# Four PSUM banks that rotate over attention units, with scores and turned probabilities of a unit in the same bank

## The reference

```python
qkv = (x @ w_qkv.T + b_qkv).reshape(B, T, 3, H, dh)
...
std_logits = jnp.einsum('bhqd,bhkd->bhqk', q, k) * scale
...
incidence = jnp.einsum('bqhp,bkhp->bhqk', read_lines, J_write)
...
weights = decays[:, None, None] ** diffs_pos[None] * past[None].astype(x.dtype)
bias = incidence * weights[None] * bias_scale[None, :, None, None]
logits = std_logits + bias
...
logits = jnp.where(causal_mask[None, None], -jnp.inf, logits)
attn = jax.nn.softmax(logits, axis=-1)
out = jnp.einsum('bhqk,bhkd->bqhd', attn, v).reshape(B, T, D)
return out @ w_out.T + b_out
```

## Time and profile before

| | |
|---|---|
| median of 3 runs | 3171.58 us (3170.65 to 3173.0) |
| the profiled execution: its time | 3169.16 us |
| the profiled execution: its span, first to last instruction | 3167.4 us |
| mean clock granted to PE | 0.789 of full speed |
| PE, DVE, ACT, POOL busy over the span | 76%, 49%, 33%, 26% |
| attention iterations | eight, from about 190 to 2085 us |

### The profile page before, as it was taken

The page is one execution under the profiler, slowest core; times in us unless marked ns, Lnnn a source line. Parts: engine busy times, 40 slices in busy tenths (PEclk is TensorE's granted clock), DMA queues, the critical chain, the costliest instruction groups (busy, mean ns, idle before and its releaser), DMA issues. The chain is left out here.

```text
span 3167.4 us, 33541 instructions
## 1 busy us (share of the span) xinstructions
PE 2413.1 (76%) x11754; PEld 1587.2 (50%) x11754; DVE 1562.1 (49%) x3728; ACT 1037.9 (33%) x2567; POOL 830.2 (26%) x583
## 2 busy tenths in 40 slices
PE   6258877777777767877777777855999597979798
PEld 5134444444444444544444444533777357574747
DVE  2468567466565765745755754422000144444443
ACT  2024343343343334334234334321222151515050
POOL 0435243153153134225224321020000223232220
PEclk9567886877777677688688688677999797979787
DMA  3000100110020010010020010022222302020200
GB/s 144 35 15 1 55 21 1 42 43 1 10 75 1 9 58 18 9 56 21 1 64 21 1 55 21 1 69 82 90 90 90 103 1 65 3 59 9 56 12 14
DMA packets 66386, 120.48 MB, mean 38 GB/s; under 512 B 29621, under 2 KB 43947, under 8 KB 63795
## 3 DMA queue, kind: packets, MB, share of 16 engines
q1 hardware_dynamic: 53434, 76.51, 7.2%
q0 software_dynamic: 12800, 41.95, 4.8%
HBM read 97.36 MB, written 21.07 MB: 37 GB/s over the span
## 5 line engine op out<-in xcount | busy, mean ns | idle before, releaser
L1022 ACT ACTIVATE att_buf<-att_buf,nmin 128x384 f32<-128x384 f32 (+3 forms) x512 | 288.3, 563 | 854.2 <-DVE nmin L1344 854.0
L858 PE MATMUL bank<-kk,qT 32*128 32x512 f32 (+2 forms) x1024 | 352.7, 725 | 92.1 <-DVE nmin L1344 92.0
L690 POOL TENSOR_TENSOR big<-ex_at,kx 128x2048 f32<-128x2048 f32 x64 | 236.6, 3705 | 428.1 <-DVE xt_na L1131 354.3
L885 PE MATMUL bank<-ident,att_buf 128*128 128x128 f32 x1280 | 254.0, 339 | 22.3 <-ACT att_buf L1030 19.2
L639 POOL TENSOR_TENSOR big<-kx 128x1280 f32<-128x1280 f32 x64 | 162.7, 2570 | 311.1 <-ACT kx L957 303.2
L1131 DVE TENSOR_REDUCE xt_na<-big 128x64 f32<-128x1024 f32 x128 | 240.8, 1899 | 2.2 <-POOL big L690 1.6
L1333 DVE TENSOR_TENSOR att_buf<-bank,wdiag 128x128 f32<-128x128 f32 x384 | 93.0, 284 | 288.9 <-PE bank L863 286.2
L899 PE MATMUL bank<-att_buf,vp 128*32 128x128 f32 x2560 | 234.0, 323 | 0.0
L1030 ACT COPY att_buf<-bank 128x384 f32<-128x384 f32 (+3 forms) x512 | 208.8, 410 | 21.8 <-PE bank L899 17.3
L885 PEld LDWEIGHTS bank<-ident,att_buf 128*128 128x128 f32 x1280 | 187.2, 179 | 33.8 <-ACT att_buf L1022 23.1
L858 PEld LDWEIGHTS bank<-kk,qT 32*128 32x128 f32 x1024 | 117.4, 234 | 165.7 <-DVE nmin L1344 124.5
(11 more groups left out here) (333 smaller groups left out, 4525.1 us busy)
## 6 DMA issues: line engine op xcount, KB each, us to landing
ew<-in_eW SPq DMA_DIRECT2D x16, 1024.0 KB, 8.4
buf_d<-gac SPq DMA_DIRECT2D x16, 320.0 KB, 2.8
eb<-buf_d SPq DMA_DIRECT2D x8, 640.0 KB, 3.6
y_d<-yy SPq DMA_DIRECT2D x8, 640.0 KB, 10.7
xt_na<-in_xT SPq DMA_DIRECT2D x8, 512.0 KB, 3.6
nA<-in_xN SPq DMA_DIRECT2D x8, 512.0 KB, 4.4
x_d<-x SPq DMA_DIRECT2D x8, 512.0 KB, 4.2
kf<-x_d SPq DMA_DIRECT2D x8, 512.0 KB, 3.2
```

Of the source, the lines that this page charges most:

```text
L690: pool.tensor_tensor(pv[:, :, c * P:(c + 1) * P].rearrange("p o (h d) -> p o h d", d=DH), spread(ex[:, t, :, 8 * c:8 * c + 8], 3, DH), spr ...
L858: pe.matmul(bank[u % 2][:, 0:n], qT[r:r + 32, g, i * P:(i + 1) * P], kk[r:r + 32, g, T * i * P:T * i * P + n], start=True, stop=False)
L885: mm = pe.transpose(bank[3 + u % 2][:, j * P:(j + 1) * P], pr[:, u % NPR, j * P:(j + 1) * P], ident[:])
L1022: act.activation(pr[:, u % NPR, 0:n], pr[:, u % NPR, 0:n], ACT.Exp, scale=-1.0, bias=nmin[:, u % 4:u % 4 + 1], accum_out=rsum[:, i, h:h + ...
```

## The change

Two banks for scores and two for turned probabilities become one ring of four, rot(u) = bank[(0, 1, 3, 4)[u % 4]]. The scores of unit u go to rot(u); when DVE has read them, turn(u) writes the turned probabilities of the same unit to the same bank. The bank is free for unit u + 4 when ACT has copied it, so scores(u) now waits for prT_ok in place of max_ok, and turn(u) loses its own wait for prT_ok.

The orders on the engines change with it. On PE: turn(k), side work, scores(k+2), values(k); scores of pairs 0 and 1 are issued ahead of the loop. On ACT: both exps of pair k, both turned of pair k, side work. On DVE the order is kept, with one more wait, for its own minima of the pair before. raw_out(0) on ACT is called one pair sooner in the count (u = 30), the sums' steps on PE stand at the end of their pair, and values of the last pair stand ahead of turn_sums(1).

```diff
--- before.py
+++ after.py
@@ -541,6 +541,8 @@
                 sm = sb("sm", [P, 16, T])
                 gi = sb("gi", [P, 4, T])
 
+                ROT = (0, 1, 3, 4)
+                rot = lambda u: bank[ROT[u % 4]]
                 units = [(2 * (2 * d + x) + c, i) for d in range(H // 4) for i in (3, 0, 2, 1) for c in range(2) for x in range(2)]
                 N = len(units)
                 long_before = [sum(i == T - 1 for _, i in units[0:u]) for u in range(N)]
@@ -567,13 +569,15 @@
                                 while pair[1] is not None and pair[1] <= slot:
                                     pair[1] = next(pair[0], None)
 
-                        def interleave(unit, streams):
+                        def interleave(unit, streams, unit_end=lambda u: None):
 
                             for u in range(0, N, 2):
                                 if b2 is not None:
                                     unit(u)
                                 advance(streams, u)
                                 advance(streams, u + 1)
+                                if b2 is not None:
+                                    unit_end(u)
                             assert all(due is None for _, due in streams)
 
                         with nc.Block() as block:
@@ -841,7 +845,7 @@
                                     g, r = row_of(u)
                                     k = long_before[u]
                                     if k >= 2:
-                                        pe.wait_ge(s("inc_used"), k - 1)
+                                        pe.wait_ge(s("inc_used"), k - k % 2)
                                     if k % 2:
                                         pe.wait_ge(s("inc_mm"), k)
                                     if u == N // 2 + 4 * T:
@@ -855,18 +859,18 @@
                                     i = units[u][1]
                                     g, r = row_of(u)
                                     n = min(i + 2, T) * P
-                                    pe.matmul(bank[u % 2][:, 0:n], qT[r:r + 32, g, i * P:(i + 1) * P],
+                                    pe.matmul(rot(u)[:, 0:n], qT[r:r + 32, g, i * P:(i + 1) * P],
                                               kk[r:r + 32, g, T * i * P:T * i * P + n], start=True, stop=False)
 
                                 def mask(u):
                                     i = units[u][1]
-                                    pe.matmul(bank[u % 2][:, i * P:(i + 1) * P], identb[:], negb[:], start=False, stop=True)\
+                                    pe.matmul(rot(u)[:, i * P:(i + 1) * P], identb[:], negb[:], start=False, stop=True)\
                                         .then_inc(s("score_mm"), 1)
 
                                 def scores(u):
 
-                                    if u >= 2:
-                                        pe.wait_ge(s("max_ok"), u)
+                                    if u >= 4:
+                                        pe.wait_ge(s("prT_ok"), u - 2)
                                     if units[u][1] == T - 1:
                                         incidence(u)
                                     logits(u)
@@ -879,10 +883,8 @@
                                 def turn(u):
                                     h, i = units[u]
                                     pe.wait_ge(s("exp_ok"), u + 1)
-                                    if u >= 2:
-                                        pe.wait_ge(s("prT_ok"), u - 1)
                                     for j in range(i + 1):
-                                        mm = pe.transpose(bank[3 + u % 2][:, j * P:(j + 1) * P], pr[:, u % NPR, j * P:(j + 1) * P], ident[:])
+                                        mm = pe.transpose(rot(u)[:, j * P:(j + 1) * P], pr[:, u % NPR, j * P:(j + 1) * P], ident[:])
                                     mm.then_inc(s("turn_mm"), 1)
 
                                 def values(u):
@@ -914,12 +916,13 @@
                                     pe.matmul(bank[2][:], sel[:], rT, start=True, stop=True).then_inc(s("rb_mm"), 1)
 
                                 def unit(u):
-                                    if u + 2 < N:
-                                        scores(u + 2)
                                     turn(u)
                                     turn(u + 1)
-                                    if u:
-                                        values(u - 2)
+
+                                def unit_end(u):
+                                    if u + 4 < N:
+                                        scores(u + 4)
+                                    values(u)
                                     if u == N // 2 + 4:
                                         turn_sums(0)
                                     if u == N // 2 + 6:
@@ -933,10 +936,10 @@
                                 if b2 is not None:
                                     turn_features()
                                     scores(0)
-                                interleave(unit, side)
+                                    scores(2)
+                                interleave(unit, side, unit_end)
                                 if b2 is not None:
                                     turn_sums(1)
-                                    values(N - 2)
                                     broadcast_sums(1)
 
                                     pe.wait_ge(s("att_ok"), 2)
@@ -1027,7 +1030,7 @@
                                     act.wait_ge(s("turn_mm"), u + 1)
                                     if u >= 3:
                                         act.wait_ge(s("val_mm"), (u - 3) // 2 + 1)
-                                    act.copy(prT[:, u % 3, 0:n], bank[3 + u % 2][:, 0:n]).then_inc(s("prT_ok"), 1)
+                                    act.copy(prT[:, u % 3, 0:n], rot(u)[:, 0:n]).then_inc(s("prT_ok"), 1)
 
                                 def raw_out(c):
 
@@ -1039,11 +1042,11 @@
                                     act.copy(rT, bank[2][0:H // 2, :]).then_inc(s("rT_ok"), 1)
 
                                 def unit(u):
-                                    for x in (u, u + 1):
-                                        if x + 2 < N:
-                                            exps(x + 2)
-                                        turned(x)
-                                    if u == N // 2:
+                                    exps(u)
+                                    exps(u + 1)
+                                    turned(u)
+                                    turned(u + 1)
+                                    if u == N // 2 - 2:
                                         raw_out(0)
                                     if u == N // 2 + 4:
                                         sums_out(0)
@@ -1073,9 +1076,6 @@
                                             last = act.activation(blocks(g, at, n), tiles_of(src, n), ACT.Copy, scale=fack[:, g, v:v + 1])
                                         last.then_inc(s("qkT_ok0"), 1)
                                 advance(side, -1)
-                                if b2 is not None:
-                                    exps(0)
-                                    exps(1)
                                 interleave(unit, side)
                                 if b2 is not None:
                                     sums_out(1)
@@ -1323,8 +1323,10 @@
                                     i = units[u][1]
                                     n = (i + 1) * P
                                     dve.wait_ge(s("score_mm"), u + 2)
+                                    if u:
+                                        dve.wait_ge(s("max_ok"), u)
                                     for x in range(2):
-                                        h, lg = units[u + x][0], bank[(u + x) % 2]
+                                        h, lg = units[u + x][0], rot(u + x)
                                         db = dpad[:, x * T * P:x * T * P + P]
                                         if i == T - 1:
                                             k = long_before[u + x] % 2
@@ -1333,7 +1335,7 @@
                                             dve.tensor_tensor(db, lg[:, n:n + P], wdiag[:, h, :], ALU.mult).then_inc(s("db_ok"), 1)
                                     tiled = lambda ap: ap.rearrange("p (j k) -> p j k", k=P)
                                     for x in range(2):
-                                        lg, dst = bank[(u + x) % 2], pr[:, (u + x) % NPR, 0:n]
+                                        lg, dst = rot(u + x), pr[:, (u + x) % NPR, 0:n]
                                         if i == T - 1:
                                             dve.wait_ge(s("inc_used"), long_before[u + x] + 1)
                                         else:
```

## The result

The kernel became slower: 3219.81 us median (3210.08 to 3232.01, 4 runs) against 3171.11 us (3164.23 to 3173.0, 4 runs); the ratio is 1.016, 95% interval 1.0121 to 1.0198. The forecast was 3154 us with a range of 3118 to 3195: the time moved the other way and lies above the range. In the changed kernel the lines stand two to four lower: scores are L862 (was L858), incidence L854 (L850), masks L867 (L863), turns L887 (L885), values L901 (L899), exponentials L1025 (L1022), copies L1033 (L1030), minima L1346 (L1344), turned router rows L767 (L763).

The account below looks back on a forecast made before the run. Attention was taken as bound by a chain alternating between PE and DVE, no engine full. Middle iterations -25, first +6, last +1 sum to -18 us: 3151.2 from the profiled 3169.2, 3154 as median; range 3118 to 3195.

Parts of the forecast that it names:

- What it adds (1): Pairs without PE side work: PE waits for ACT's copies before the next scores, 0.57 us each.
- Seven or eight of the 17 lie under DVE's stretch and cost nothing: Middle iteration: of 17 pairs without PE side work, those where DVE is full add nothing; the other 9 cost 5 us.
- the broadcast: Sums' broadcast (L914) on PE comes later; DVE waits 1.3 to 3.4 us for it in its full stretch, 2.5 taken.
- What it saves: Attention: scores no longer wait for the pair before's biases, some 1.5 us saved at one pair; iteration start gains about 1.4.
- The walk of the middle iteration: Operations of 657 to 863 us replayed in the new order at old durations: 4.1 us saved, 25 over six iterations.
- The first iteration: Attention without router: 22 us of turnarounds and other additions replace 16.2 us of waits; it loses 6 us.
- The last iteration: Attention without token mixing: 19 turnarounds (11 us) and 3 us of moved outputs against 8.1 + 4.5 of waits; loses about 1.
- The moved outputs: Raw output holds turns of unit 16 about 1.3 us; later sums' broadcast makes DVE's L1320 wait, 2.5 us taken.
- The window named as the test: Middle attention window: prediction is wrong if its granted clock moves by more than 0.03 from 0.74.
- Rival B: Attention: the clock falls, three more pairs per iteration at the lower level, 41 us over the forecast, 3195; chance 0.11.
- The other sign: Attention on DVE: prediction is wrong if DVE's idle time ahead of the biases does not shrink.
- A: Attention: turnaround not repaid, 93 us added against 73 saved, 20 us slower, 3191; chance 0.17.

Follow-up runs that it names:

- e2: Changed kernel with a prT ring of four and values of the pair before right behind the turns: 3105.76 us, ratio 0.9791.
- e8: Changed kernel with every copy of turned probabilities made twice, one after the other: 3404.98 us, ratio 1.0733.
- e11: e2 with prT back as a ring of three: 3207.34 us, ratio 1.012.
- e5: Changed kernel unaltered, run again on another chip: 3226.92 us, ratio 1.0165.
- e10: Changed kernel with ACT's order altered: copies, then exponentials of the next pair, then side work: 3199.63 us, ratio 1.0114.
- e1: Changed kernel with values of a pair ahead of the next scores in place of behind them: 3185.45 us, ratio 1.0038.
- e6: Changed kernel with prT as a ring of four, all else as changed: 3214.34 us, ratio 1.0137.
- e3: Kernel before the change with values of the pair before moved between the next scores and the turns: 3177.29 us, ratio 1.0025.
- e7: Kernel before the change with prT as a ring of four, all else as before: 3178.31 us, ratio 1.0013.
- e9: e2 with ACT's exponentials of the next pair between the copies and the side work: 3127.79 us, ratio 0.9864.

## Why the prediction was wrong

**The step that failed** is "What it adds (1)", the turnaround, priced as waiting alone. The forecast charged 0.57 us to 102 pairs (29 in the first iteration, 9 in each middle one, 19 in the last), 58 us, and let PE's busy time stand still: "every operation at the duration that it has there", "I take the mean granted clock as unchanged". The wait itself was right (0.53 us, 138 times). PE's idle time in the attention part even fell by 33 us, where the whole forecast is -18; but its busy time, put at no change, grew by 60.5, and -33 + 60.5 = 27.5 us is what came. By the estimate above some 35 of the 60.5 are the lower clock and 25 the lost overlap of the turns' and the masks' ends.

What an uncovered turnaround costs in all is after against e2 (ring and order of values together): 98 us, 45 of idling and 53 of busy time. The 53 go with the clock and not with the overlap. PE is busy 773 us at the lower level in after and 662 in e2, 744 and 801 at the upper one: 111 us less there and 58 more here, and at 1.8 to one that is the same work within 5 us.

"Seven or eight of the 17 lie under DVE's stretch and cost nothing" failed too: that stretch took 49.5 us in place of 45.0, where the forecast had 2.5 for the broadcast, and e8 lengthened it by 4.0 more.

**What it saves** fits what came. The forecast's net of -18 us without its 58 us of turnarounds is -76; e2, with the turnaround covered, has an attention part 70.6 us shorter than before, though with another order and another clock, so part of this fit may be luck. In the changed kernel PE's idle time fell by 6.5 us in a middle iteration, more than the 4.1 of the walk; the busy time took it back, and 242.2 became 242.4.

**The walk of the middle iteration.** Means over the six, each mark counted from its iteration's first projection: the lead at the first side work behind a pair was 1.6 us (predicted 1.5 after pair 0); 2.7 at the side work of pair 10 (predicted 5.6); 6.8 at the router's turned rows (8.6); 3.8 in DVE's full stretch, where 5.2 to 7.7 were expected; 0.6 behind pair 28; -0.2 at the end. So the shape held (the gain comes with the square root's chain, and is lost in the stretch and in the last pairs), with 1.4 to 4.3 us less at the marks from pair 10 on.

**The first iteration** was to lose 6 us. Its idle time grew by 6.3, its busy time by another 7.1. Window and waits of the changed kernel, for the earlier trace rows:
```profile
223.00:378.00 155.00, 127.01 (x732) 70.25 (x732) 92.01 (x240) 68.04 (x203) 51.76 (x24) 0.71 0.00 1
```
```profile
PE bank L862 <- ACT att_buf L1033: 12.4, 22, 0.7
PE bank L887 <- ACT att_buf L1025: 5.0, 4, 2.0
...
PE bank L854 <- ACT att_buf L1033: 2.9, 6, 0.5
```
The same stretch of e11 has as much idling (28.5 us against 28.0) at a clock of 0.77, and is 12 us shorter:
```profile
223.00:366.00 143.00, 114.52 (x732) 64.52 (x732) 91.29 (x239) 69.30 (x202) 51.78 (x24) 0.77 0.00 1
```
Over the whole first iteration PE is busy 75 us at the lower level before, 81 in after and 59 in e11. By the same 1.8 to one, of the 7.1 us of busy time that the change added here some 4.5 are lost overlap and 2.6 the clock, and of the 12 us by which e11 is shorter some 9 are the clock.

**The last iteration** was to lose 1 us and lost 2.1 (12.6 in e5). **The moved outputs**: L1320 on DVE waits 2.7 to 7.3 us more for L916 in the three middle iterations that were read (2.5 taken), and 45 us more over all eight. **The gaps** between iterations, which the forecast left out, grew by 10.8 us: the output projection, 3.72 us long at the end of all eight iterations before, took 5.23 to 5.41 with the same matmuls.

**The clock.** The window named as the test has 0.74 in both kernels, so that sign of being wrong didn't show, by luck of the window: over the attention part the clock went from 0.763 to 0.745 (0.76 and 0.75 in the views), and in later middle iterations by up to 0.04 (0.77 to 0.73 in the iteration shown above). The Trainium skill, "TensorE: Matmul & The Clock Gate", section "A second HAM failure mode: psum-queue depth-cycling", has brief idling between groups of matmuls cost throughput by way of the clock, and the trace agrees in direction. Rival B's 41 us are near the 35 estimated here, so B is a part of what happened. It isn't all: e2 and e10, at 0.77 both, differ by 95 us, 85 of it idle time. The fall goes along with exposed turnarounds (0.74 to 0.75 in after, e1, e5, e6 and e11, 0.69 with the copies doubled; 0.76 or 0.77 in before, e3, e7, e2 and e9), but e10 exposes them and has 0.77. What brings the clock down is not shown.

**The other sign did show.** The prediction was to be wrong "if DVE's idle time ahead of B does not shrink". It didn't: 440.4 us before, 446.1 after, and 365.9 in e2.

**Of the rivals**, A is what came, with another working: the score waits went wholly and not by half, and the turnaround, with what it does to order and clock, cost more than they gave. It decides where the prediction put it, at the middle iteration: e2 gives back 11.2 us there, after none.

**Open:** the attention part explains 27 to 37 us (after, e5, e6) of median differences of 48 to 60 us. The rest of the profiles' difference lies behind it, mostly in unchanged layer 1 code, and was not traced to the change. How the loss divides between wait, overlap and clock is an estimate; no run holds the clock still.

## What to carry to other kernels

When two uses of a PSUM bank are joined, the bank's way back (here turns, copy, next scores) becomes a link on PE's own path: count it at every group, at the wait plus the lost overlap and with an eye to the clock, not at the wait alone, and put independent matmuls behind the group that the copy reads. Check that the cover is free of the same loop: the values used as cover freed the copy's own target buffer, so one more slot was needed, and neither cover nor slot was worth much without the other. A sum made of waits alone misses what PE's busy time does; compare it, iteration by iteration, in the trace, and set the runs' times beside their granted clocks before taking one profile for the kernel.

## What the runs showed of the hardware

A pass of layer 1, the same code in all kernels, takes 160 us, and in some profiles 10 us more. Windows of the first and second pass in the changed kernel:
```profile
2563.52:2735.20 171.68, 149.85 (x609) 107.05 (x609) 65.92 (x140) 49.87 (x82) 42.34 (x34) 0.78 0.11 32
2735.20:2895.32 160.12, 138.00 (x608) 98.21 (x609) 65.97 (x140) 49.81 (x82) 42.36 (x34) 0.83 0.11 34
```
The surplus is PE's busy time (149.9 against 138.0 us) at a lower granted clock (0.78 against 0.83), with DVE's and ACT's work the same. The end of the span, from the fourth pass on, is 10 us longer in the same way (164.4 us here, 154.2 before). The surplus always stands in one of these two places. Over the 13 profiles the first pass took 159.6 to 162.3 us in seven and 169.1 to 172.1 in six (after, e2, e5, e6, e7, e11), the last 152.1 to 154.2 in nine and 164.4 or 164.5 in four (after, e1, e5, e7); the two passes between never took over 161.8. Both profiles of the changed kernel have both, but so has e7, which is before with a ring of four, and e8 and e10, which have the new banks, have neither. So it isn't bound to this change alone, and what brings it on stays open. What lies outside the attention part varies from 1272.6 to 1297.3 us over the 13 profiles of this study, though its code is the same. A single profile of such a kernel can't be asked for differences under 0.8%.
